# Where the query product stands in a slot of an attention pipeline

## The reference

```
q = (xn @ Wq).reshape(b, n, H, DH).transpose(0, 2, 1, 3) * scale
k = concat([null_k, xn @ Wk]);  v = concat([null_v, xn @ Wv])
sim = einsum('bhid,bjd->bhij', q, k) + bias
attn = softmax(where(causal_mask | key_mask, neg, sim))
out = einsum('bhij,bjd->bhid', attn, v) @ Wo
```

## Time and profile before

| what | value |
|---|---|
| median of 3 runs | 1049.11 us (1048.52 to 1057.35) |
| span of the profiled execution | 1055.2 us |
| PE busy | 932.6 us, 88% of the span |
| VectorE (DVE) busy | 803.2 us, 76% |
| ScalarE (ACT) busy | 735.9 us, 70% |
| GpSimd (POOL) busy | 606.0 us, 57% |

### The profile page before, as it was taken

The page is one execution under the profiler, slowest core; times in us unless marked ns, Lnnn a source line. Parts: engine busy times, 40 slices in busy tenths (PEclk is TensorE's granted clock), DMA queues, the critical chain, the costliest instruction groups (busy, mean ns, idle before and its releaser), DMA issues. The chain is left out here.

```text
span 1055.2 us, 22432 instructions
## 1 busy us (share of the span) xinstructions
PE 932.6 (88%) x6180; PEld 811.6 (77%) x6180; DVE 803.2 (76%) x2324; ACT 735.9 (70%) x1651; POOL 606.0 (57%) x699
## 2 busy tenths in 40 slices
PE   7899999999999999999999966887976762599997
PEld 5578888888888898998888755677964652499996
DVE  7579989899898898998888879774757786344443
ACT  2268888888888998998999937434764652466663
POOL 2368777777776666775555525481066277344444
PEclk8879999999999999999999986888988885699999
DMA  9156656666666566675665440155864523254453
GB/s 309 44 175 180 189 171 189 178 181 180 176 184 182 170 197 182 187 199 167 182 189 171 137 150 1 51 167 148 282 178 157 205 102 138 88 78 78 73 84 48
DMA packets 111427, 162.14 MB, mean 154 GB/s; under 512 B 16201, under 2 KB 85193, under 8 KB 110282
## 3 DMA queue, kind: packets, MB, share of 16 engines
q1 hardware_dynamic: 100200, 140.56, 45.1%
q0 software_dynamic: 10224, 18.00, 8.2%
q10 hardware_dynamic: 882, 2.14, 0.6%
HBM read 110.31 MB, written 25.17 MB: 128 GB/s over the span
## 5 line engine op out<-in xcount | busy, mean ns | idle before, releaser
L2375 POOL TENSOR_SCALAR probs<-probs,inv_sum 128x1024 f32<-128x1024 f32 (+3 forms) x128 | 301.7, 2370 | 174.2 <-DVE inv_sum L2526 174.2
L2421 ACT ACTIVATE probs<-probs,neg_max 128x1025 f32<-128x1025 f32 (+7 forms) x256 | 197.5, 772 | 30.9 <-DVE neg_max L2486 29.8
L2508 DVE TENSOR_TENSOR pT_lo<-t_ps,pT_hi 128x512 fp32r<-128x512 f32 (+1 forms) x320 | 202.5, 633 | 21.3 <-ACT pT_hi L2403 20.8
L2590 PE MATMUL t_ps<-ident,probs 128*128 128x128 f32 x1152 | 179.9, 274 | 1.1 <-DVE pT_lo L2508 1.1
L2610 PE MATMUL o_ps<-pT_hi,values 128*128 128x256 f32 x576 | 175.0, 323 | 5.2 <-DVE pT_lo L2508 3.5
L2403 ACT ACTIVATE pT_hi<-t_ps 128x512 fp32r<-128x512 f32 (+1 forms) x320 | 175.5, 549 | 5.5 <-PE t_ps L2590 2.3
L2486 DVE CUSTOM_DVE_ANT_0 probs<-s_ps,bias_set,neg_null 128x512 f32<-128x512 f32 (+3 forms) x256 | 164.2, 642 | 4.5 <-PE s_ps L2559 2.6
L2590 PEld LDWEIGHTS t_ps<-ident,probs 128*128 128x128 f32 x1152 | 141.9, 141 | 31.4 <-DVE pT_lo L2508 2.7
L2611 PE MATMUL o_ps<-pT_lo,values 128*128 128x256 f32 x576 | 150.4, 281 | 0.0
L2558 PE MATMUL s_ps<-k_hi,q_hilo 128*128 128x512 f32 (+3 forms) x384 | 143.8, 375 | 4.2 <-PEq L2730 1.4
L2559 PE MATMUL s_ps<-k_lo,q_one 128*128 128x512 f32 (+3 forms) x384 | 135.4, 353 | 0.0
(11 more groups left out here) (385 smaller groups left out, 2124.7 us busy)
## 6 DMA issues: line engine op xcount, KB each, us to landing
bias_set<-bias_dram SPq DMA_DIRECT2D x16, 1024.0 KB, 5.5
bias_set<-bias_dram SPq DMA_DIRECT2D x16, 896.0 KB, 5.4
bias_set<-bias_dram SPq DMA_DIRECT2D x16, 768.0 KB, 4.9
bias_set<-bias_dram SPq DMA_DIRECT2D x16, 640.0 KB, 4.7
q_hilo<-q_hi SPq DMA_DIRECT2D x128, 64.0 KB, 2.0
q_hilo<-q_lo SPq DMA_DIRECT2D x128, 64.0 KB, 2.0
q_one<-q_hi SPq DMA_DIRECT2D x128, 64.0 KB, 2.0
bias_set<-bias_dram SPq DMA_DIRECT2D x16, 512.0 KB, 5.5
```

Of the source, the lines that this page charges most:

```text
L2375: last = pool.tensor_scalar(keys, keys, inv_sum[:, x.set, unit, h:h + 1], None, ALU.mult)
L2421: act.activation(p, p, ACT.Exp, scale=-1.0, bias=neg_max[:, x.set, row.unit, h:h + 1], accum_out=row_sum[:, x.set, row.unit, h:h + 1]).the ...
L2508: dve.tensor_tensor(pT_lo[n % 3][:, 0:count, :], t_ps[TURNS["slot", n] % 3][:, 0:2 * P * count].rearrange("p (n q) -> p n q", n=count), pT ...
L2590: last = pe.transpose(t_ps[at % 3][:, P * (2 * m + h):P * (2 * m + h) + P], probs_row(x, row, h)[:, 1 + P * (k + m):1 + P * (k + m) + P], ...
```

## The change

The items of each slot from 0 on are sorted so that a query product stands first. This touches slot 2 alone: its list becomes q, s3, and `RING` numbers them in this order. VectorE takes an item ahead of its low part only where the first item of the list is a score chunk.

```
 SCORES_AT[-1].sort(key=lambda item: ...)
+for _n in range(NS):
+    SCORES_AT[_n].sort(key=lambda item: item[0] != "q")
 RING = {item: i for i, item in enumerate(item for n in range(-1, NS) for item in SCORES_AT[n])}
...
                 for n in range(NS + 1):
-                    for item in SCORES_AT.get(n, ())[:1]:
+                    items = SCORES_AT.get(n, ())
+                    early = 1 if items and items[0][0] == "s" else 0
+                    for item in items[:early]:
                         fill(item)
                     low(n + 1)
-                    for item in SCORES_AT.get(n, ())[1:]:
+                    for item in items[early:]:
                         fill(item)
```

## The result

The changed kernel takes 1087.7 us (median of 4 runs, 1086.76 to 1090.82), the kernel before beside it 1049.94; the ratio is 1.034 (95% interval 1.0295 to 1.0385). It is slower, as forecast, but by 3.4% where 2.5% was said: 1087.7 lies above the range of 1062 to 1085. The granted clock is 1.00 from 66 us to the end of the attention stage in both kernels, so the clock has no part in it.

A forecast was written before the change was run, and what follows sets the result against it. VectorE's work plus its pauses in slots 2 and 3 was taken to bound each step. Middle steps summed to 27.4 us, round ends to -1.4: +26.0 on 1049.1, say 1075 us, range 1062 to 1085.

The forecast's parts named there:

- VectorE's wait for q: Slot 2: with q first on PE, VectorE's wait for its high part, 23.4 us in all, goes in every round.
- s3 came on top: Slot 2, rounds 4 to 7: low(3) starts where it did, and s3's time is added behind it.
- the clock stayed: Attention rounds: PE's clock stays 1.00; the rival, a falling clock, gave 1084 us, chance 0.06.
- The first steps of a round: Seven first steps, where VectorE waits 0.87 us for q: the new order gains some 0.3 us each.
- VectorE's wait for PE at s4: At s4: new waits for PE, about 0.4 us in rounds 4 and 5, more in 6 and 7.
- The last steps of rounds: Seven last steps, where q waited too: the new order costs only about +0.1 us each.
- The upper bound of +37: Whole change: PE hand-over at 0.20 us, 0.1 more a step from ScalarE's line, first steps gaining nothing: about +37 us.
- The sample step of rounds 0 and 1: Step 12, taken for 13 steps of rounds 0 and 1: +0.56 us each, with q's wait of 0.43 gone.
- That is 0.12 us more.: Slot 2 on VectorE: s3's wait for q just issued costs 0.12 us against a pair without such a wait.
- The hand-over from PE: From PE's end to the reader's start at s4: 0.10 us, bounds 0.03 and 0.20.
- PE's own return: From q's read to s4's product done: 0.06 + 0.34 + 0.39 = 0.79 us for 512 columns, 0.69 for 384.
- That was s3, read early; now it is q: S4's bank, rounds 4 to 7: PE starts s4 only after q's read; +0.87 and +0.93 us a step.

The follow-up runs named there:

- e3: Changed kernel, but s3 waits on VectorE for s2's read instead of q's: 1079.86 us, ratio 1.0268.
- e2: Kernel before with VectorE's low(3) ahead of s3 and nothing else, PE and banks as before: 1083.75 us, ratio 1.0313.
- e6: Changed kernel with ScalarE scaling the short row behind the query, in slot 2 instead of slot 1: 1054.42 us, ratio 1.0037.
- e8: Changed kernel with s3 waiting for s2 alone, low(4) ahead of s4 on VectorE, and the short row scaled behind the query: 1053.46 us, ratio 1.0014.
- e7: Kernel before with q right behind s3 on PE, and the short row scaled behind the query from round 4 on: 1074.44 us, ratio 1.0202.
- e5: Kernel before with q right behind s3 on PE, ahead of project and turn: 1073.02 us, ratio 1.02.
- e10: Kernel before with e9's order only in rounds 0 to 3 and rounds' first and last steps; short row later in steps without q: 1046.61 us, ratio 0.9917.
- e9: Kernel before with q between project and turn on PE, VectorE's order and banks as before: 1050.23 us, ratio 0.9972.

## Why the prediction came out too low

**What held.** VectorE's wait for q went; low(3) stayed where high(3) lets it be; s3 came on top; PE waited for q's read before s4 and VectorE for PE; `invert` waited longer in rounds 0 and 1; rounds 2 and 3 paid least; the clock stayed. The first steps of a round gained (1.9 us over seven, 7 x 0.3 = 2.1 said). Two signs were off in size: rounds 0 and 1 lost as much a step as rounds 4 to 7, not half, and VectorE's wait for PE at s4 is 0.16 us in rounds 4 and 5, not about 0.4, because s3 itself starts 0.22 us late.

**What failed are sizes.** By rounds, predicted and measured a step: 0.56 and 1.02, 0.11 and 0.28, 0.87 and 0.96, 0.93 and 1.05. With the same counts that is 13 x 1.02 + 12 x 0.28 + 12 x 0.96 + 9 x 1.05 = 37.6 us where 27.4 stood. The last steps of rounds cost 1.6 us over seven, not 0.7. Together that is 37.6 + 1.6 - 1.9 = 37.3 of the 37.7 us measured. The upper bound of +37 was nearly met; the range had taken only a part of it.

- *The sample step of rounds 0 and 1.* Step 12 waits 0.43 us for q; its neighbours wait 0.16, as step 11 above, and last 8.51 us against its 8.78. The 0.27 us that it had to lose were taken as if every step had them: 13 x 0.27 = 3.5 us too little. The trace of before held this; one more step read beside it would have shown it. Step 12 itself went from 8.78 to 9.54 us.
- *"That is 0.12 us more."* The price of s3's wait behind q was read from a pair of other instructions. It measured 0.22 us of idle and the lost overlap of 0.08, so 0.30 in all: 0.18 more in each of 25 steps, 4.5 us. e3 takes it out again and gets 0.31 and 0.24 us. The Trainium skill says that a semaphore after each operation costs nothing extra ("VectorE: DVE Perf Modes", section "The DRAIN you can't avoid"). For this pair the trace speaks against it: 0.30 us. The 13 x 0.18 and 13 x 0.27 together are the 6 us by which rounds 0 and 1 were short.
- *The hand-over from PE.* 0.10 us was taken from q's way to ScalarE, with 0.20 as the upper bound; in step 36 it measured 403.96 - 403.77 = 0.19. That is all of the 0.09 us missing in rounds 4 and 5 and 0.09 of the 0.12 in rounds 6 and 7. PE's own return was right: 0.06, then 0.28 between the products, then 0.34. The Trainium skill says that PE can pull weight loads ahead of matmuls in flight ("TensorE: Matmul & The Clock Gate", section "Architectural detail: the array is 16× 32×32, not 1× 128×128"). In this trace the load of s4's first product isn't pulled ahead of the wait: it starts at 403.15, with its product; that of the second starts at 403.26, while the first product runs.

The last two prices were in the trace of before, on the same instruction. At 46.05, still ahead of step 0, a second chunk waits for the chunk just before it on VectorE and starts 0.22 us after that one's end (45.75 + 0.08 = 45.83), and in round 5 an s4 waits for PE (product done at 467.23 + 0.40 = 467.63) and starts 0.19 us later:

```profile
45.75 0.08 DVE L2486 DVE_READ_ACCUMULATOR2_ANT part_max<- 128x1 f32 x1
46.05 0.75 DVE L2486 CUSTOM_DVE_ANT_0 probs<-s_ps,bias_set,part_max 128x512 f32<-128x512 f32 x1 [0.22 <-DVE part_max L2486]
...
467.23 0.40 PE L2559 MATMUL s_ps<-k_lo,q_one 128*128 128x512 f32 x1
...
467.82 0.75 DVE L2486 CUSTOM_DVE_ANT_0 probs<-s_ps,bias_set,neg_null 128x512 f32<-128x512 f32 x1 [0.18 <-PE s_ps L2559]
```

Another instruction of VectorE starts 0.04 us after PE's last product there, at the same clock of 1.00 (861.32 + 0.24 = 861.56, then 861.60):

```profile
861.32 0.24 PE L201 MATMUL pa_logits_ps<-rt_chosen,rt_ones 128*128 128x8 bf16 x4
...
861.60 0.19 DVE L209 TENSOR_TENSOR rt_base<-pa_logits_ps,rt_carry 128x32 f32<-128x32 f32 x1 [0.40 <-PE pa_logits_ps L201]
```

So both prices go with the chunk instruction, which starts about 0.2 us after its release, be it by VectorE or by PE, and not with the pair of engines; the prediction had read them from other instructions.

**The attribution.** The prediction put the late s4 of rounds 4 to 7 on the numbering of the banks ("That was s3, read early; now it is q"). This step failed, though the number didn't depend on it: e2 shows that with the old numbering s4 is as late, behind s3's read, because s3 is no longer read early. Whichever item VectorE reads first behind low(3) holds the bank of s4.

**What stays open.** Why the custom chunk instruction, with two waits and a counter update in front, starts 0.19 to 0.22 us after its release, and the pair of the earlier trace rows after 0.04, wasn't tried. It isn't the only one that starts late: L2058, VectorE's in a later stage, starts 0.27 us behind PE's product (919.42 + 0.29 = 919.71, then 919.98, in the trace of before). Whether the short row scaled behind the query would make the kernel before faster by itself wasn't run either: e6 and e8 have it on top of the change, e7 on top of e5, where PE is late, and e10 in the last steps alone. How much of what e6 and e8 win back would have been won without the change as well is therefore not known. The last steps of rounds and step 0, which alone costs 2.2 us more, weren't taken apart.

## What to carry to other kernels

An engine that is on the path should do the thing it can do now while it waits for the thing it can't: moving the consumer of a late result to the front exposes that result's whole delay. When items share two buffers in turn, changing their order changes for whom each next one waits; write down item e and e-2 for every edit, on the writer as well (it was missed twice here, in e5 and e9). After an edit look for new waits as well as for the one that shrank (e10). And read a cost from an instruction of the same kind, in an ordinary step: search the whole trace for that instruction behind a wait, and take three neighbouring steps and see that they agree before one of them is multiplied.

## What the runs showed of the hardware

- VectorE's chunk instruction (L2488) that waits for the instruction just before it on the same engine starts 0.22 us after that one's end, in nearly every step the same; a plain pair started after 0.04 us, one with no such wait 0.08 us before the end.
- From the modelled end of PE's product to the start of the chunk instruction on it there are 0.19 us at a granted clock of 1.00 (403.77 to 403.96), to another instruction of VectorE 0.04 (861.56 to 861.60), from q's product to ScalarE 0.10.
- The attention stage repeats to 0.2 us between executions (548.0 and 547.8), while the stages behind it took 443.2 and 434.7 us in the same kernel.
